# The state of a chunked scan kept as two halves of the heads, on 64 rows each

## What is computed

```python
zxbcdt = u @ W_in + b_in                 # z, xs (8 heads x 64), Bm (64), Cm (64), dt (8)
dt = softplus(zxbcdt[..., -8:] + dt_bias)
decay = exp(dt * A)
def step(h, inp):                        # h: heads x 64 x state 64
    h = dec_t[:, :, None, None] * h + dtx_t[..., None] * B_t[:, None, None, :]
    y = einsum('bhpn,bn->bhp', h, C_t)
y = y + D_skip * xs
out = (y * silu(z)) @ W_out + b_out
```

## Time and profile before

| what | value |
|---|---|
| runs, median (lowest to highest) of 3 | 1644.97 us (1644.22 to 1649.27) |
| profiled execution: span from first to last instruction | 1640.7 us |
| around the span, against the median | 4.3 us |
| mean granted TensorE clock | 0.991 |
| busy PE, DVE, ACT, POOL | 95%, 73%, 48%, 35% of the span |
| the scan's 32 jobs, by the start of L2757 | 857.0 to 1161.3 us |

### The profile page before, as it was taken

The page is one execution under the profiler, slowest core; times in us unless marked ns, Lnnn a source line. Parts: engine busy times, 40 slices in busy tenths (PEclk is TensorE's granted clock), DMA queues, the critical chain, the costliest instruction groups (busy, mean ns, idle before and its releaser), DMA issues. The chain is left out here.

```text
span 1640.7 us, 25927 instructions
## 1 busy us (share of the span) xinstructions
PE 1565.0 (95%) x9320; PEld 1359.8 (83%) x9320; DVE 1202.6 (73%) x2680; ACT 787.8 (48%) x1578; POOL 578.1 (35%) x474
## 2 busy tenths in 40 slices
PE   6999989999999999999988999999799999999997
PEld 4689878988989888867877889888688788898896
DVE  6776688876668657655988899999778747666763
ACT  3333333455467245427257787778411325444442
POOL 2100020000000012320536878777300034777764
PEclk9999999999999999999989999999999999999999
DMA  7000000000020000212134223322232135665653
GB/s 237 5 1 1 1 1 27 1 27 1 1 103 27 14 5 16 94 58 85 34 106 158 80 81 92 89 81 81 77 133 63 39 100 152 159 160 137 162 108 39
DMA packets 81174, 116.35 MB, mean 71 GB/s; under 512 B 15724, under 2 KB 60312, under 8 KB 80152
## 3 DMA queue, kind: packets, MB, share of 16 engines
q1 hardware_dynamic: 67096, 96.21, 18.2%
q0 software_dynamic: 12288, 17.31, 5.9%
q10 hardware_dynamic: 1664, 1.18, 0.2%
HBM read 86.37 MB, written 27.68 MB: 70 GB/s over the span
## 5 line engine op out<-in xcount | busy, mean ns | idle before, releaser
L2120 POOL DMA_INDIRECT k_xe<-rows_dram,idx x64 | 82.5, 1289 | 174.7 <-DVE idx L3463 140.5
L2899 POOL DMA_INDIRECT out<-k_eo,idx x64 | 117.0, 1828 | 73.1 <-DVE k_eo L2993 58.8
L1948 PE MATMUL d_pO<-d_sp,d_raw 128*128 128x257 f32 x512 | 114.6, 380 | 3.3 <-DVE x L1330 3.2
L1948 PEld LDWEIGHTS d_pO<-d_sp,d_raw 128*128 128x128 f32 x512 | 95.6, 189 | 17.7 <-DVE x L1330 4.1
L583 ACT ACTIVATE b_p<-b_pS,b_nmax 128x384 f32<-128x384 f32 (+16 forms) x32 | 38.1, 1192 | 128.2 <-DVE b_nmax L725 128.2
L61 PE MATMUL b_pO<-b_vh,b_ph 128*128 128x256 f32 x302 | 87.7, 291 | 5.1 <-DVE b_pl L706 5.1
L63 PE MATMUL b_pO<-b_vl,b_ph 128*128 128x256 f32 x302 | 85.3, 283 | 0.0
L62 PE MATMUL b_pO<-b_vh,b_pl 128*128 128x256 f32 x302 | 85.3, 282 | 0.0
L373 POOL TENSOR_TENSOR x<-x,b_vrow 128x256 f32<-128x256 f32 x32 | 24.4, 792 | 163.3 <-DVE b_hs L652 163.2
L2354 ACT ACTIVATE g_dlm<-d_cumb,mod 128x128 f32<-128x128 f32 x256 | 78.6, 400 | 0.7 <-DMA d_cumb<-cum_dram 0.7
L2953 ACT ACTIVATE k_act_g<-i_pg 128x512 f32<-128x512 f32 x64 | 38.3, 598 | 83.5 <-PE i_pu L63 83.2
(11 more groups left out here) (590 smaller groups left out, 5450.1 us busy)
## 6 DMA issues: line engine op xcount, KB each, us to landing
d_cumb<-cum_dram SPq DMA_DIRECT2D x32, 512.0 KB, 4.2
k_wf<-in_WgT SPq DMA_DIRECT2D x16, 512.0 KB
k_wf<-in_WuT SPq DMA_DIRECT2D x16, 512.0 KB
k_wf<-in_WdT SPq DMA_DIRECT2D x16, 512.0 KB
rows_dram<-h_hx SPq DMA_DIRECT2D x32, 136.0 KB, 3.8
x<-in_x SPq DMA_DIRECT2D x8, 512.0 KB, 9.8
d_w<-in_w SPq DMA_DIRECT2D x4, 1024.0 KB, 6.2
uT_dram<-d_ug SPq DMA_DIRECT2D x16, 256.0 KB, 2.4
```

What stands on the lines that cost most here:

```text
L1948: last = nc.tensor.matmul(pO[:, t % 2, 0:PW], raw[e][:, t * P:(t + 1) * P], proc[e], start=e == 0, stop=e == E - 1)
L2120: nc.gpsimd.indirect_dma_start(out=m.xe[:, e % 2, t, :], out_offset=None, in_=m.rows, in_offset=bass.IndirectOffsetOnAxis(ap=column(m, e, ...
L2899: nc.gpsimd.indirect_dma_start(out=out, out_offset=bass.IndirectOffsetOnAxis(ap=column(m, e, t), axis=0), in_=eo[:, e % 2, t, :], in_offse ...
```

## The change

H is kept on all 128 partitions with 256 columns: heads 0 to 3 on rows 0 to 63, heads 4 to 7 on rows 64 to 127. `states` is cut in two. `recall(n)` reads the state by two products of 64 contraction rows and 256 columns: rows 0 to 63 write `pi[:, 0:256]`, rows 64 to 127 write `pst[:, 256:512]` (another bank). The new `states(n)` makes the new part by two products of 128 contraction rows, 64 output rows and 256 columns, onto rows 0 to 63 and 64 to 127 of `pst[:, 0:256]`; it runs after `within(n)` and waits for `t1_done`. VectorE's two operations on H have the shape 128x256 where it was 64x512, and `update(n)` runs after `gates` and `sums(n)`. C is copied twice side by side so that its transpose stands on both halves of the rows; ScalarE has one copy more for it. The table of total decays has a half of the heads on each half of the partitions. The diff's core:

```diff
-        H = sb("g_H", [P, B, INNER])
+        H = sb("g_H", [P, B, INNER // 2])
+        sb("g_H_rest", [P, B, INNER // 2])
-        py, pi, pst, pyT = [ps("g_p" + n, [P, 512]) for n in ("y", "i", "st", "yT")]
+        py, pip, pyT = ps("g_py", [P, 512]), ps("g_pip", [P, 1024]), ps("g_pyT", [P, 512])
+        pi, pst = pip[:, 0:512], pip[:, 512:1024]
@@ scalar
-                nc.scalar.copy(bc[:, b, :, 0:STATE], pbc.rearrange("p (k n) -> p k n", k=2)).then_inc(s["bc_copied"], 1)
+                nc.scalar.copy(bc[:, b, 0, 0:STATE], pbc[:, 0:STATE])
+                nc.scalar.copy(bc[:, b, 1].rearrange("p (a n) -> p a n", a=2), over(pbc[:, STATE:2 * STATE], 2)).then_inc(s["bc_copied"], 1)
@@ vector
-                nc.vector.tensor_tensor(heads(y[:, b]), heads(pi[:]), wide(cs[:, b, 2]), ALU.mult).then_inc(s["t1_done"], 1)
+                nc.vector.tensor_tensor(halved(y[:, b]), from_state, by_half(cs[:, b, 2]), ALU.mult).then_inc(s["t1_done"], 1)
-                nc.vector.tensor_tensor(heads(H[0:STATE, b]), heads(H[0:STATE, b]), wide(et[:, b], STATE), ALU.mult).then_inc(s["hs_done"], 1)
+                nc.vector.tensor_tensor(half_heads(H[:, b]), half_heads(H[:, b]), half_wide(et[:, b]), ALU.mult).then_inc(s["hs_done"], 1)
-                nc.vector.tensor_tensor(H[0:STATE, b], H[0:STATE, b], pst[0:STATE, :], ALU.add).then_inc(s["h_done"], 1)
+                nc.vector.tensor_tensor(H[:, b], H[:, b], pst[:, 0:INNER // 2], ALU.add).then_inc(s["h_done"], 1)
-                if is_job(n):
-                    update(n)
                 if n == 0:
                     last_residual(1, 2)
                 if n >= PRIMED - 1 and is_job(n + 1):
                     gates(n + 1)
                 if is_job(n):
                     sums(n)
+                    update(n)
@@ tensor
-            def states(n):
+            def recall(n):
                 b = n % B
                 pe.wait_ge(s["h_done"], n)
                 pe.wait_ge(s["t1_done"], n)
                 pe.wait_ge(s["hT_copied"], max(n - 3, 0))
+                pe.wait_ge(s["s_copied"], max((n - 5) // B, 0))
...
-                nc.tensor.matmul(pi[:], bcT[:, b, 1, :], H[:, b], start=True, stop=True).then_inc(s["i_ready"], 1)
...
+                for half, dst in zip(HALVES, (pi[:, 0:INNER // 2], pst[:, INNER // 2:INNER])):
+                    last = nc.tensor.matmul(dst, bcT[half.rows, b, 1, :], H[half.rows, b], start=True, stop=True)
+                last.then_inc(s["i_ready"], 1)
+
+            def states(n):
+                b = n % B
+                pe.wait_ge(s["xw_done"], n + 1)
+                pe.wait_ge(s["t1_done"], n + 1)
+                for half in HALVES:
+                    last = nc.tensor.matmul(pst[half.rows, 0:INNER // 2], bc[:, b, 0, 0:STATE], xw[:, b, half.cols], start=True, stop=True)
+                last.then_inc(s["st_ready"], 1)
...
-                    states(n)
+                    recall(n)
                 if n == 3:
                     late_turn()
                 if is_job(n + 1):
+                    await_bc(n + 1)
                     state_rows(n + 1)
                 if is_job(n):
                     within(n)
+                    states(n)
```

More of the change, by code:

```diff
@@ L2 @@
 from concourse import mybir
+from collections import namedtuple
 from contextlib import ExitStack
@@ L872 @@
 INNER = 2 * C
+Half = namedtuple("Half", "rows heads cols")
+HALVES = [Half(slice(a * STATE, (a + 1) * STATE), slice(a * HEADS // 2, (a + 1) * HEADS // 2), slice(a * INNER // 2, (a + 1) * INNER // 2))
+          for a in range(2)]
 HD = INNER // HEADS
@@ L929, in soft_mixture @@
         m.bias, m.u0 = placed("bias", [P, DT0], kept + 24 * KB), placed("u0", [P, B, CH, P], kept + 29 * KB)
-        m.etot = placed("etot", [STATE, NT, HEADS], kept + 31 * KB)
+        m.etot = placed("etot", [P, NT, HEADS // 2], kept + 31 * KB)
         m.wogl, m.wogh = placed("wogl", [P, B, INNER // P, C], kept + 32 * KB, FR), placed("wogh", [P, B, INNER // P, C], kept + 40 * KB, FR)
@@ L1760, in decay_sums @@
                 nc.scalar.activation(ecum_[:, tiles], decay_bank(k, 0).rearrange("p (t h) -> p t h", h=HEADS), ACT.Exp)
-                nc.scalar.activation(m.etot[:, tiles].rearrange("p t h -> p (t h)"), decay_bank(k, 2)[0:STATE], ACT.Exp)
+                for half in HALVES:
+                    nc.scalar.activation(m.etot[half.rows, tiles], decay_bank(k, 2)[half.rows].rearrange("p (t h) -> p t h", h=HEADS)[:, :, half.heads],
+                                         ACT.Exp)
                 act.wait_ge(s["f_chain"], CHAIN * k + 1)
@@ L1977, in cumulate @@
                 nc.tensor.matmul(decay_bank(k, 1), m.after[:], dA, start=True, stop=True)
-                nc.tensor.matmul(decay_bank(k, 2)[0:STATE], m.ones[:, 0:STATE], dA, start=True, stop=True).then_inc(s["f_cum"], 1)
+                nc.tensor.matmul(decay_bank(k, 2), m.ones[:], dA, start=True, stop=True).then_inc(s["f_cum"], 1)
             def turn_sums(k):
@@ L2145, in state_space @@
         px = ((slice(0, P), m.pL[:, X_AT:X_AT + P]), (slice(P, INNER), slabs[2]))
-        py, pi, pst, pyT = [ps("g_p" + n, [P, 512]) for n in ("y", "i", "st", "yT")]
+        py, pip, pyT = ps("g_py", [P, 512]), ps("g_pip", [P, 1024]), ps("g_pyT", [P, 512])
+        pi, pst = pip[:, 0:512], pip[:, 512:1024]
+        from_state = pip[:].rearrange("p (a n) -> p a n", n=INNER // 2)[:, 0:4:3, :].rearrange("p a (h d) -> p a h d", d=HD)
         po = pyT[:, 0:C]
@@ L2158, in state_space @@
         pT, pg, pS = pi[:, 0:CH * P], py[:, 0:EX], pst[:, 0:P]
-        f_pc, f_ps, f_pt, f_pT = pst[:, P:P + NL], pst[:, 2 * P:2 * P + NL], pst[0:STATE, 3 * P:3 * P + NL], pbt[0:NL, 3 * P:4 * P]
+        f_pc, f_ps, f_pt, f_pT = pst[:, P:P + NL], pst[:, 2 * P:2 * P + NL], pst[:, 3 * P:3 * P + NL], pbt[0:NL, 3 * P:4 * P]
         staged = lambda n: (n + 1) // B * 48
@@ L2176, in state_space @@
         heads = lambda t: t.rearrange("p (h d) -> p h d", h=HEADS)
-        wide = lambda col, p=P: col.unsqueeze(2).to_broadcast([p, HEADS, HD])
+        wide = lambda col: col.unsqueeze(2).to_broadcast([P, HEADS, HD])
+        halved = lambda t: t.rearrange("p (a h d) -> p a h d", a=2, d=HD)
+        by_half = lambda col: col.rearrange("p (a h) -> p a h", a=2).unsqueeze(3).to_broadcast([P, 2, HEADS // 2, HD])
+        half_heads = lambda t: t.rearrange("p (h d) -> p h d", d=HD)
+        half_wide = lambda col: col.unsqueeze(2).to_broadcast([P, HEADS // 2, HD])
         NJ = NTB * B
@@ L2397, in late_sums @@
                 nc.scalar.activation(ecum_, f_pc.rearrange("p (t h) -> p t h", h=HEADS), ACT.Exp)
-                nc.scalar.activation(m.etot[:, late].rearrange("p t h -> p (t h)"), f_pt, ACT.Exp)
+                for half in HALVES:
+                    nc.scalar.activation(m.etot[half.rows, late], f_pt[half.rows].rearrange("p (t h) -> p t h", h=HEADS)[:, :, half.heads], ACT.Exp)
                 act.wait_ge(s["f_chain"], 1)
@@ L2455, in _ @@
         def _(dve):
-            nc.vector.memset(bc[:, :, :, STATE:P], 0.0).then_inc(s["zeroed"], 1)
+            nc.vector.memset(bc[:, :, 0, STATE:P], 0.0).then_inc(s["zeroed"], 1)
             def low(n):
@@ L2754, in states @@
                 pe.wait_ge(s["hT_copied"], max(n - 3, 0))
+                pe.wait_ge(s["s_copied"], max((n - 5) // B, 0))
                 if n == 0:
                     pe.wait_ge(s["zeroed"], 2)
-                nc.tensor.matmul(pi[:], bcT[:, b, 1, :], H[:, b], start=True, stop=True).then_inc(s["i_ready"], 1)
[L2758 to L2761, removed]
                 if n == 3:
                     pe.wait_ge(s["f_kept"], 1)
-                nc.tensor.matmul(pst[:], bc[:, b, 0, :], xw[:, b], start=True, stop=True).then_inc(s["st_ready"], 1)
+                for half, dst in zip(HALVES, (pi[:, 0:INNER // 2], pst[:, INNER // 2:INNER])):
[5 more added lines that the diff above has]
+                pe.wait_ge(s["t1_done"], n + 1)
+                for half in HALVES:
+                    last = nc.tensor.matmul(pst[half.rows, 0:INNER // 2], bc[:, b, 0, 0:STATE], xw[:, b, half.cols], start=True, stop=True)
+                last.then_inc(s["st_ready"], 1)
             def within(n):
@@ L2814, in late_cumulate @@
                 nc.tensor.matmul(f_ps, m.after[:], f_dA[:], start=True, stop=True)
-                nc.tensor.matmul(f_pt, m.ones[:, 0:STATE], f_dA[:], start=True, stop=True).then_inc(s["f_cum"], 1)
+                nc.tensor.matmul(f_pt, m.ones[:], f_dA[:], start=True, stop=True).then_inc(s["f_cum"], 1)
             def late_turn():
@@ L3532, in program @@
             m.csb = m.mod[:, 1, GA, 0:B * 4 * 8].rearrange("p (b k h) -> p b k h", b=B, k=4)
-            m.etb = m.mod[0:64, 1, GA, B * 4 * 8:B * 5 * 8].rearrange("p (b h) -> p b h", b=B)
+            m.etb = m.mod[:, 1, GA, B * 4 * 8:B * 4 * 8 + B * 4].rearrange("p (b h) -> p b h", b=B)
             banks = ctx.enter_context(ExitStack())
```

## The result

The changed kernel takes 1676.82 us (median of 4 runs, 1671.96 to 1678.23), and the kernel before, run beside it, 1644.60. The ratio is 1.0188 (95% interval 1.0162 to 1.0215): 31 us slower (32 between the medians), where I predicted 8, and outside my range of 1638 to 1664. The page's head stands against the earlier trace rows: the span has grown by 35.7 us, and TensorE's busy time by 16 of them.

The account below looks back on a forecast made before the run. TensorE was taken to bound the scan: 0.43 us gained and 0.60 paid a step, +5.1 us in 30 steps, plus 2.8 for head and tail, made 1644.97 + 7.9 = 1653 us; range 1638 to 1664.

Parts of the forecast that it names:

- The moves: `states` behind `within`, `update` behind `gates` and `sums`: nothing in mid-scan, at most 0.3 us in 16 steps for the range.
- Which covers most: ScalarE's second copy, some 0.25 us more a step, was held mostly covered by its 1.8 us a step of waiting.
- Half beside half with a quarter lost: Each pair of half-array products on TensorE takes 0.64 us instead of 0.85, gaining 0.43 us a step.
- rival 1: TensorE's halves run fully side by side, 0.43 us a pair instead of 0.85: 1640 us, or 1634 with cheap form changes; chance 0.22.
- the order in the queue: On TensorE both records of the first half go ahead, so the second half starts beside the first half's second record.
- The form change: Switching TensorE to another array form and back costs 0.30 us for each pair, 0.60 us a step.
- head and tail: Waits outside mid-scan: +0.5 us in step 1, +1.5 in step 2, +0.8 in the last job, together +2.8 us.
- the point where VectorE begins to count: VectorE's 0.75 us a step saved stays hidden, counting only if TensorE gets shorter by more than 0.5 us a step.
- the 0.2 us that I gave `by_expert` to spare: In even steps `by_expert` waits on TensorE for `update`, which was to end with 0.2 us to spare, so costed at nothing.

Follow-up runs that it names:

- experiment 1: The kernel before with the change's order alone (`states` behind `within`, `update` behind `sums`), no halves and no second copy of C: 1673.15 us, ratio 1.0166.
- experiment 4: The changed kernel with ScalarE's second copy of x cut in two, one more copy ahead of h_ex: 1677.24 us, ratio 1.0193.
- experiment 3: The changed kernel with ScalarE making h_ex right behind its copies of x, ahead of the tanh and bias copy: 1648.48 us, ratio 1.0021.
- experiments 2 and 3: The same earlier h_ex on ScalarE in two kernels: 2 in that of experiment 1, without halves, 1653.49 us (1.0059); 3 in the changed kernel, 1648.48 us.
- Experiment 5: The changed kernel with `states` back ahead of `within` from job 1 on, halves and shared bank kept: 1668.22 us, ratio 1.0145.

## Why the prediction was wrong

**The step that failed is "The moves".** There I followed what the moved piece itself waits for (`sums`, `update`, `by_expert`) and costed the middle of the scan at nothing. I didn't ask what the piece had stood over. `within` waits for h_ex as well, and this wait is in none of my lists. The trace of before showed no idle time for it, because the 0.86 us of L2764 lay on it with 0.28 us to spare. From rows of before it could have been priced: h_ex ends 1.65 us after `recall` starts, and without L2764, and with my own 0.64 us for `recall`, `within` would be due at 1.93 - 0.86 - 0.21 = 0.86. That is 0.8 us of waiting in an odd step, and by the even steps' 1.35 us some 0.5 in those: about 19 us in 30. Measured: 17.2 us of idle time for h_ex in 28 steps, and in experiment 1 0.67 us a step in the middle and 29 us in all, low clocks included.

**ScalarE.** "Which covers most" read the same thing wrongly. I took ScalarE's mean wait of 1.8 us a step for slack of the whole engine. It lies ahead of the copies; between the copies and h_ex ScalarE has none (no idle time at L2384 in the timeline above), and an addition there reaches `within`, as the 0.06 us of experiment 4 did. The second copy of the change was small, though: h_ex comes 0.10 us later against `logits` than before (in step 20: 1.89 us for 1.79), and `recall` comes 0.09 later too.

**The halves.** Half beside half with a quarter lost, 0.64 us without form changes, was wrong too: rival 1's mechanism holds. From a pair's first record to the next group's first it takes 0.63 (`recall`) and 0.59 us (`states`), part of the form change included. Narrow cuts of PE's timeline show how. The first is of 1080.200 to 1080.252, the second of 1080.200 to 1080.258, the third of 1080.75 to 1080.85, all of the kernel after:

```profile
1080.25 0.48 PE L2776 MATMUL g_pip<-g_H,g_bcT 64*128 64x256 f32 x1
```

```profile
1080.25 0.49 PE L2776 MATMUL g_pip<-g_H,g_bcT 64*128 64x256 f32 x2
```

```profile
1080.57 0.38 PE L2776 MATMUL g_pip<-g_H,g_bcT 64*128 64x256 f32 x2
```

One record has started by 1080.252 and two by 1080.258; the two records' starts are 7 ns apart. The other two are together as well, 0.32 us later; by the ends that the profile models (1080.73 and 1080.95) the two pairs are 0.22 us apart, what 256 columns take. So the records don't run as first half twice and then second half twice, as I had argued from the order in the queue; they run as two pairs side by side.

The Trainium skill ("TensorEngine Tiling (Array Packing)", Key Properties) says that tiles work independently of each other and can run in parallel; the trace agrees, 7 ns against the 0.21 us that I took.

**The form change** was nearly right. Beside each other the columns of both pairs take 2 x 0.43 = 0.85 us less than before; the cheapest step got 0.21 us shorter (9.30 in experiment 3, 9.51 before), so some 0.64 us went into form changes, 0.32 a pair, where I took 0.30. The Trainium skill ("TensorEngine Tiling (Array Packing)", Key Properties) says that a change of the tiling mode drains the engine; the trace agrees: L2776 starts 0.57 us after L2761 (L2757 0.48 after L2747 before), and L2745 0.63 us after L2776, whose columns take 0.43. With 0.21 us gained in each of 30 steps, and the 2.8 of my head and tail, the sum would have been 1641, rival 1's case. Even steps would have kept less of it: 9.55 us in experiment 3 against 9.61 before, as `by_expert` waits for `update` there.

**VectorE** gained (busy 27 to 23 us in 30), and in the kernel after nothing came of it, as I said. But that held only because `within` waited for h_ex. With this wait gone, `update` sets when an even step goes on, and its shorter time on 128 rows is part of what the halves gave between experiments 2 and 3. I had put the point where VectorE begins to count at 0.5 us less a step on TensorE; it came with 0.2, and the 0.2 us that I gave `by_expert` to spare were none in experiment 3.

**Head and tail.** Steps 0 to 4 cost 2.0 us, the 2.0 predicted, but by luck. `late_cumulate` in step 2 waited 2.05 us instead of 0.65, 1.4 more, where I had 1.5; but a stretch at half clock followed it. Step 1, which I had 0.5 us longer, took 9.29 us for 12.98: its wait of 1.92 us and the lower clock behind it (0.51 in 873:876 before) were gone. Step 0 took 1.4 us more, with a wait of 2.59 us ahead of `states` that I had not listed. `recall` of the last job waited 2.68 us for `keep_scores` where L2764 had waited 1.45: 2.3 us in step 30, and 3.3 behind the last `recall`, where I had 0.8 for both.

**The clock** was in none of my terms. The four stretches in steps 5, 24, 27 and 29 cost, beside the waits ahead of them, 1.5 + 3.1 + 3.1 + 3.2 = 10.9 of the 35.7 us. The one in step 2 cost some 2.9 (15.12 us for 10.87, less 1.4 of waiting), but stands against the one in step 1 that only the kernel before has. What the lower clock behind the last `recall` cost was not separated.

## What to carry to other kernels

When a piece is moved on the engine that bounds the kernel, list every wait of the instruction that now comes sooner, and read in the trace when each of its releasers ends; a wait with no idle time in front of it is not one with slack, and the piece that you take away may be its whole cover. Slack of a helping engine holds for a place in its order: its idle time ahead of a chain doesn't help what is late at the end of the chain. And behind an idle time of 1.4 us on TensorE the lower clock cost up to 3.2 us more here, though not each time, so a wait should be priced with and without that.

## What the runs showed of the hardware

Two float32 products on different halves of the array start 7 ns apart and interleave by record, though each has two records, and a pair of 2 x 256 columns holds the engine for 0.59 to 0.63 us, from its first record to the next group's. Changing form costs about 0.3 us a pair: 0.43 us of columns saved by each of two pairs, and 0.21 us off the step.

The clock behind an idle time isn't settled by its length alone. After 2.05 us of idle time in step 2 the kernel after has the lower level (0.50) in 886:892; experiment 4 with 2.06 us at the same place keeps the full clock:

```profile
886.00:892.00 6.00, 5.37 (x23) 5.40 (x24) 2.38 (x10) 2.92 (x8) 1.59 (x2) 0.50 1.02 294
```

```profile
886.00:892.00 6.00, 6.00 (x42) 5.80 (x44) 3.94 (x12) 2.71 (x11) 2.48 (x2) 1.00 0.98 325
```

The kernel before idled 1.45 us in its last job and had 1.00 in 1162:1168. Experiment 5 idled 1.72 and 1.74 us in steps 27 and 29 at 1.00; experiment 1 idled 1.37 us in the same two steps and had 0.57 in 1152:1156 but 1.00 in 1178:1184; experiment 4 idled 0.98 us in steps 9 and 11 and fell only behind the second (0.50 in 981:987). What else decides was not tried and stays open.
